# Base products with high and low weights as one 512-column matmul in a routed low-rank layer on Trainium2

## The reference

```python
base = jnp.einsum('btd,od->bto', x, W)
logits = jnp.einsum('btd,ed->bte', x.astype(jnp.float32), Wr.astype(jnp.float32))
logits = logits + bias[:, None, :]
topw, topi = jax.lax.top_k(logits, TOP_K)
weights = jax.nn.softmax(topw, axis=-1)
gates = jnp.sum(jax.nn.one_hot(topi, E, dtype=weights.dtype) * weights[..., None], axis=-2)
h = jnp.einsum('btd,erd->bter', x, A)
lora_out = jnp.einsum('bter,bte,eor->bto', h, gates, B)
return base + SCALING * lora_out      # and x is added to it
```

## Time and profile before

| | us |
|---|---|
| median of 3 runs | 79.89 (79.57 to 80.69) |
| profiled execution | 79.78 |
| its span, first to last instruction | 78.0 |
| PE busy (502 matmuls) | 74.6 |
| PE weight loads busy | 70.8 |
| VectorE busy (220 instructions) | 48.5 |
| ScalarE, GpSimd busy | 22.4 each |

### The profile page before, as it was taken

How to read it: one execution, slowest core, us unless ns; L and a number is a source line. 1 busy time by engine, 2 the same in 40 slices (tenths; PEclk the granted TensorE clock), 3 DMA queues, 4 the chain that set the end, 5 groups by cost and what they waited for, 6 DMA issues and landing times.

```text
span 78.0 us, 1627 instructions
## 1 busy us (share of the span) xinstructions
PE 74.6 (96%) x502; PEld 70.8 (91%) x502; DVE 48.5 (62%) x220; ACT 22.4 (29%) x57; POOL 22.4 (29%) x26
## 2 busy tenths in 40 slices
PE   5999999999999999999999999999999999999960
PEld 2269999899999999999999999999999999999950
DVE  0097587878864828283755829283755739787750
ACT  1743941514502314140504113140404023122100
POOL 4053725064160514124060605123060606000000
PEclk9999999999999999999999999999999999999999
DMA  1999994499389389999920000350000072032143
GB/s 13 317 312 358 424 413 192 50 384 380 48 303 429 60 274 420 437 248 377 415 95 0 0 0 0 167 236 0 0 0 0 0 296 107 0 134 97 42 139 135
DMA packets 4037, 14.24 MB, mean 183 GB/s; under 512 B 448, under 2 KB 1472, under 8 KB 3776
## 3 DMA queue, kind: packets, MB, share of 16 engines
q1 hardware_dynamic: 3744, 13.65, 47.8%
q10 hardware_dynamic: 288, 0.53, 1.9%
HBM read 9.99 MB, written 4.19 MB: 182 GB/s over the span
## 4 chain that ended last, share of the span: by engine, by line
PE 96%; DVE 1%; issue 0%
PE heads_ps L436 43%; PE base_ps L436 28%; PE heads_ps L476 5%; PE base_ps L476 5%; PE warm_ps L509 4%; PE base_ps L480 2%; PE heads_ps L480 2%; PE ghT_ps L467 2%; PE heads_ps L514 2%; PE base_ps L460 2%; DVE out_sb L428 1%; PE warm_ps L467 0%
## 5 line engine op out<-in xcount | busy, mean ns | idle before, releaser
L209 POOL TENSOR_TENSOR x_lo<-xT_sb,x_hi 128x512 fp32r<-128x512 f32 x14 | 18.1, 1294 | 38.2 <-ACT x_hi L244 36.8
L436 PE MATMUL heads_ps<-w_hi,x_hi 128*128 128x392 f32 x63 | 22.7, 368 | 0.0
L436 PE MATMUL heads_ps<-w_lo,x_hi 128*128 128x392 f32 x63 | 20.9, 340 | 0.0
L436 PE MATMUL heads_ps<-w_hi,x_lo 128*128 128x392 f32 x63 | 20.8, 342 | 0.0
L436 PE MATMUL base_ps<-w_hi,x_lo 128*128 128x256 f32 x60 | 16.6, 283 | 0.0
L436 PE MATMUL base_ps<-w_hi,x_hi 128*128 128x256 f32 x60 | 16.6, 288 | 0.0
L436 PE MATMUL base_ps<-w_lo,x_hi 128*128 128x256 f32 x60 | 16.3, 280 | 0.0
L301 DVE TENSOR_TENSOR ghT_lo<-ghT_ps,ghT_hi 128x128 fp32r<-128x128 f32 x15 | 4.4, 291 | 14.8 <-ACT ghT_hi L248 14.7
L248 ACT ACTIVATE ghT_hi<-ghT_ps 128x128 fp32r<-128x128 f32 x15 | 4.1, 275 | 29.5 <-PE ghT_ps L467 29.5
L436 PEld LDWEIGHTS heads_ps<-w_hi,x_hi 128*128 128x128 f32 x63 | 11.8, 190 | 0.8 <-issue 0.3
L436 PEld LDWEIGHTS base_ps<-w_hi,x_hi 128*128 128x128 f32 x60 | 11.5, 193 | 0.4 <-ACT w_hi L237 0.3
(11 more groups left out here) (53 smaller groups left out, 99.9 us busy)
## 6 DMA issues: line engine op xcount, KB each, us to landing
x_sb<-in_x SPq DMA_DIRECT2D x4, 768.0 KB, 5.5
out<-out_sb SPq DMA_DIRECT2D x4, 768.0 KB, 4.3
xT_sb<-in_xT SPq DMA_DIRECT2D x3, 768.0 KB, 4.2
xT_sb<-in_xT SPq DMA_DIRECT2D x1, 1024.0 KB, 6.4
x_sb<-in_x SPq DMA_DIRECT2D x1, 1024.0 KB, 9.4
first_sb<-in_first SPq DMA_DIRECT2D x2, 454.0 KB, 5.6
out<-out_sb SPq DMA_DIRECT2D x2, 256.0 KB, 2.1
out<-out_sb SPq DMA_DIRECT2D x4, 128.0 KB, 1.8
```

Source lines behind the costliest of these rows:

```text
L209: nc.gpsimd.tensor_tensor(x_lo[:, s, :], xT_sb[:, t - len(FIRST), :], x_hi[:, s, :].bitcast(FP32), ALU.subtract).then_inc(x_lo_made, 1)
L436: return nc.tensor.matmul(dst, xs[:, s, chunks[k]], ws[:, k, cols], start=(k == 0 and n == 0), stop=(k == KC - 1 and n == last_n))
```

## The change

The high and low weights become the two halves of one tensor, w_parts (and b_parts for B). Products with w_lo and w_hi that have the same stationary operand x_hi are now one matmul whose moving operand is both halves, 2 x 256 columns, and whose result fills the whole bank base_ps: high products in columns 0 to 255, low ones in columns 256 to 511. The product of x_lo with w_hi stays 256 columns wide, into the first half, and comes first in its chunk. For tiles 2 to 13 base is computed this way, and the products of ghT_hi with b_hi and b_lo for the base half too. Tiles 0, 1, 14 and 15 are as before. VectorE adds the low half to x_sb into out_sb, and then adds the high half to out_sb: two instructions of 128x256 where there was one, the second waiting for the first by the new semaphore low_added.

```diff
-        w_hi = sb("w_hi", [P, KC, WIDTH], FP32R)
-        w_lo = sb("w_lo", [P, KC, WIDTH], FP32R)
+        w_parts = sb("w_parts", [P, KC, 2, WIDTH], FP32R)
+        w_hi, w_lo = w_parts[:, :, 0, :], w_parts[:, :, 1, :]
...
-        b_hi = sb("b_hi", [ER, O], FP32R)
-        b_lo = sb("b_lo", [ER, O], FP32R)
+        b_parts = sb("b_parts", [ER, 2, O], FP32R)
+        b_hi, b_lo = b_parts[:, 0, :], b_parts[:, 1, :]
...
+            def low_onto_x(t, s, landed, count):
+                dve.wait_ge(lora_base_done, t + 1)
+                dve.wait_ge(landed, count)
+                nc.vector.tensor_tensor(out_sb[:, t, 0:BASE], base_ps[s][:, BASE:2 * BASE], x_sb[:, t, 0:BASE],
+                                        ALU.add).then_inc(low_added, 1)
+
+            def out_base_apart(t, s):
+                dve.wait_ge(low_added, t - len(FIRST) + 1)
+                nc.vector.tensor_tensor(out_sb[:, t, 0:BASE], base_ps[s][:, 0:BASE], out_sb[:, t, 0:BASE],
+                                        ALU.add).then_inc(out_made, 1)
...
-                out_rest(t - 1, before, landed, count)
-                out_base(t - 1, before)
+                if first:
+                    out_rest(t - 1, before, landed, count)
+                    out_base(t - 1, before)
+                else:
+                    out_rest(t - 1, before, landed, count)
+                    low_onto_x(t - 1, before, landed, count)
+                    out_base_apart(t - 1, before)
...
-            step(2, 2, x_group, 16)
+            step(2, 2, x_group, 16, first=True)
...
-            out_base(t0, s0)
+            low_onto_x(t0, s0, x_last, 16)
+            out_base_apart(t0, s0)
...
+            def base_apart(s, ks):
+                for k in ks:
+                    base_product(s, k, 2, first_n=2)
+                    last = nc.tensor.matmul(
+                        base_ps[s][:, 0:2 * BASE].rearrange("p (a n) -> p a n", n=BASE), x_hi[:, s, chunks[k]],
+                        w_parts[:, k, :, base_cols], start=False, stop=(k == KC - 1), skip_group_check=True)
+                return last
...
-                    for dst, cols, _ in halves:
+                    for dst, cols, _ in halves[:1] if apart else halves:
                         nc.tensor.matmul(dst, ghT_hi[s][:, :], bs[:, cols], start=False, stop=False,
                                          skip_group_check=True)
+                if apart:
+                    nc.tensor.matmul(base_ps[s][:, 0:2 * BASE].rearrange("p (a n) -> p a n", n=BASE), ghT_hi[s][:, :],
+                                     b_parts[:, :, 0:BASE], start=False, stop=False, skip_group_check=True)
...
-                base(s, (0, 1, 2))
-                lora(t - 1, before)
-                base(s, (3,)).then_inc(base_done, 1)
+                base_apart(s, (0, 1, 2))
+                lora(t - 1, before, apart=True)
+                base_apart(s, (3,)).then_inc(base_done, 1)
...
-            base(2, (0, 1))
+            base_apart(2, (0, 1))
...
-            base(2, (2, 3)).then_inc(base_done, 1)
+            base_apart(2, (2, 3)).then_inc(base_done, 1)
...
-            lora(t0, s0)
+            lora(t0, s0, apart=True)
```

More of the change, by code:

```diff
@@ L142, in cond_resid_program @@
         out_made = sem("out_made")
+        low_added = sem("low_added")
         last_x_placed = sem("last_x_placed")
@@ L352, in out_base, with step @@
                                         ALU.add).then_inc(out_made, 1)
-            def step(t, j, landed, count):
+            def low_onto_x(t, s, landed, count):
[7 more added lines that the diff above has]
+                                        ALU.add).then_inc(out_made, 1)
+            def step(t, j, landed, count, first=False):
                 s, before = j % SLOTS, (j - 1) % SLOTS
@@ L431, in _, with product @@
         def _(pe):
-            def product(dst, s, cols, k, n, last_n=2):
+            def product(dst, s, cols, k, n, last_n=2, first_n=0):
                 xs = x_lo if n == 2 else x_hi
@@ L436, in product, with base_product @@
                 return nc.tensor.matmul(dst, xs[:, s, chunks[k]], ws[:, k, cols],
-                                        start=(k == 0 and n == 0), stop=(k == KC - 1 and n == last_n))
+                                        start=(k == 0 and n == first_n), stop=(k == KC - 1 and n == last_n),
+                                        skip_group_check=first_n == 2)
             def heads_product(s, k, n, last_n=2):
                 return product(heads_ps[s][:, 0:HEADS], s, heads_cols, k, n, last_n)
-            def base_product(s, k, n):
-                return product(base_ps[s][:, 0:BASE], s, base_cols, k, n)
+            def base_product(s, k, n, first_n=0):
+                return product(base_ps[s][:, 0:BASE], s, base_cols, k, n, first_n=first_n)
             def heads(s, ks):
@@ L467, in transpose, with lora @@
                 nc.tensor.transpose(dst[:, 0:P], gh[s][:, :], ident[:, :]).then_inc(transposed, 1)
-            def lora(t, s, heads_done_only=False):
+            def lora(t, s, heads_done_only=False, apart=False):
                 halves = ((heads_ps[s][:, 0:REST], slice(BASE, O), lora_heads_done),
```

## The result

The changed kernel takes 80.16 us in the median of 22 runs, against 79.84 us for the kernel before in as many runs of the same comparison: the ratio is 1.0047, with a 95% interval of 1.0027 to 1.0066. That is 0.3 us slower by the medians and 0.4 by the ratio, far inside the 2% that count as no difference. Ratios and intervals leave out slow executions, more than 1.5% above the fastest of the same kernel; medians include them. The range of the prediction (78.9 to 80.4) holds the result, but the prediction had a small gain (-0.13 us), and that sign is outside the interval.

The account below looks back on a forecast made before the run. PE was taken to bound the kernel. Matmul savings of 0.49 us and a tail wait of 0.36 gave -0.13 on the profiled 79.78 us, 79.65; with the median 0.11 higher 79.76, given as 79.7, range 78.9 to 80.4.

Parts of the forecast that it names:

- PE bounds the kernel, VectorE has cover in the loop: Whole kernel: PE carries 96% of the chain; VectorE's extra 0.51 us a tile falls into idle time in steps 3 to 12.
- Term one: Matmuls of tiles 2 to 13: each merged pair saves 8.4 ns, 58 pairs counted, -0.49 us.
- two of the pairs are swallowed in tile 2: Tile 2's transpose waits for VectorE's gh, so two of the 60 pairs probably bring no gain.
- Its bounds: Price of a wide matmul: 213.3 ns at the clock, saving 23.3 a pair, up to 236.6, saving nothing.
- two runs cost as two matmuls: Rival on wide matmuls: each run pays the fixed part, no gain, only the tail wait; 80.25 us, chance 0.12.
- The case at the clock's rate: Rival on wide matmuls: they stream at 2.4 GHz, saving up to 23.3 ns a pair; 78.9 us, chance 0.14.
- Term two: Tail: VectorE's second addition for tile 12 makes PE wait ahead of heads of tile 15, +0.36 us.
- The two tail delays overlap and don't add: Tile 15: additions for tile 13 delay gh, but PE's transposing load has itself moved by 0.3 us, so nothing comes on top.
- The tail wait doesn't come: Rival: step 13's gate goes first, heads of tile 15 don't wait, last transpose about +0.23 late; 79.6 us, chance 0.15.
- a lock for the first to start: Step 13: VectorE and GpSimd lock a port pair against each other, the first to start holding it to the end.
- Sum: Whole kernel: -0.49 + 0.36 = -0.13 us against the profiled 79.78 us, giving 79.65.
- forecast: Main case: wide matmuls cost only the line's price and the tail wait comes; chance 0.52.

Follow-up runs that it names:

- the chains: Behind the last matmul of the kernel with one-run weights, chains of 24 matmuls of one width, a line each: 233 ns a matmul at 512 columns.
- VectorE's edit alone: Kernel before, with VectorE adding the high half a second time, dependent, for tiles 2 to 13: 80.18 us, ratio 1.0024.
- the run without the first: Changed kernel with GpSimd's last subtraction made to wait for gate of tile 13: 79.95 us, ratio 1.0014.
- widths: Behind the last matmul of the kernel with one-run weights, chains of 12 matmuls of one width, all sharing one line: 233 ns at 512 columns.

## Why the prediction was wrong

- *PE bounds the kernel, VectorE has cover in the loop:* right. The second addition cost nothing in the loop (a step of 4.360 with it alone), and ghT_lo still waits 0.95 us.
- *Term one, 58 x 8.4 = -0.49 us:* this is the step that failed. The sign held (PE saves a little by each merge), the size didn't: the wide matmul was priced at 228.2 ns and measured 233 to 234. The step became 4.347 us where 4.32 was forecast; 11 steps gave 0.14 us, 60 pairs about 0.16, 2.6 to 3 ns a pair. Whether two of the pairs are swallowed in tile 2 was not measured. The prediction drew a line through two widths, 176.7 at 392 and 118.3 at 256, which gave 0.429 ns a column and a fixed part of 8.4 ns. By the chains a line from 288 to 512 has 0.448 and 4 ns. The two rows were each within 3 ns of that line; carried from 136 columns' distance over 120 more, and with a gain that is itself a difference of near-equal numbers, this grew to 5 ns, most of the term. More care with the two rows would not have been enough: a line through the chains of 288 and 480 columns still gives 230 at 512, since the price steps up more there.
- *Its bounds:* they held the value. The case "two runs cost as two matmuls" (0.12) had nearly the right time, 80.25, but by luck and for a wrong reason: one run of 512 columns costs the same 233 ns, so it is not the second run that costs but the columns themselves. The case at the clock's rate (0.14) was much farther off, 78.9.
- *Term two, +0.36 us at the start of tile 15:* right in place and mechanism; measured +0.31 in the changed kernel and +0.34 with VectorE's edit alone. Of its parts, the second addition came 0.45 behind the first, not 0.51, and the hand-over from the output to PE's weight load took 0.11 (68.20 to 68.31), not 0.05. The two errors of 0.06 cancel, which is luck: the load was 0.41 late (68.31, where the rhythm had it at 67.90), as forecast.
- *The two tail delays overlap and don't add:* right, as the run without the first shows (7.96 instead of 8.17, not 7.86). The rival's +0.23 for the second alone was 0.12.
- *The tail wait doesn't come (0.15):* it didn't happen. Gate of step 13 took 1.32 to 1.34 us in all nine traces in which GpSimd was left as it was. The prediction's remark that the rows at 65.04 and 65.06 agree with a lock for the first to start is too strong, since they show gate first, and gate was the one held.
- *Sum:* with both terms at their measured size, -0.16 + 0.31 = +0.15 us, slightly slower. The forecast -0.13 lay on the other side of zero because one term was three times too large. That the direction of a sum so small hung on 5 ns a matmul should have been said: "no gain" and "forecast" were no two cases with 0.12 and 0.52 but two ends of one uncertain price.

## What to carry to other kernels

Merging two matmuls that share their stationary operand saved only 3 ns of 237 here, where they run back to back, while splitting the sum over two halves of a bank costs an addition of 0.45 us a tile on another engine. Look for the one tile where that engine has no cover, since it decides. Before a price is extended from two neighbouring widths, work out what 1 or 2 ns on either point make of it; a chain of matmuls behind the kernel's last one measures it in one execution. And an instruction that takes six times its usual time in one step (gate, 1.32 us) marks where slack is gone, before any change is made.

## What the runs showed of the hardware

- In the reduced float32 form, with the granted clock at 1.00 and a weight load for each matmul, 288 columns cost 133 ns and 512 cost 233, 0.448 ns a column on average with about 4 ns beside; in bfloat16 it is 0.41 a column with 219 ns at 512.
- At 256 columns float32 came to 118 ns in the kernel and 114 in a chain. At 128 and 192 it came to 112 in widths, where bfloat16 at 128 columns came to 59.
- A moving operand in two runs of 256 columns costs what one of 512 does, 233 ns.
- A dependent addition of 128x256 on VectorE starts 0.45 us behind the one whose result it reads (27.11 to 27.56), an independent one 0.33 to 0.34.
- The 128x8 gate on VectorE took 1.32 to 1.34 us beside a GpSimd subtraction of 128x512 shown to start 0.02 us later, and 0.23 when the subtraction came 0.12 us or more behind it.
- In VectorE's straight-line code a gap of 0.2 to 0.4 us, without a wait for another engine, stood at the same place in two traces of the same kernel. Its cause is open.
